# Routing slots of a two-branch layer: row units, wide comparisons, and a shifted job pair

## The reference

```python
xn = _layernorm(x, axis=-1)
x = x + attn(xn, ...) + ffn(xn, ...)

# attention branch: 16-channel tokens, qkv, windows of 8, depthwise conv, projection, norm
qkv = (tok @ qkv_w).reshape(B, -1, 3, C)
out = softmax(q * scale @ k.T) @ v + lepe
# expert branch: 16 experts in 4 groups, the best 6 of the best 2 groups
scores = sigmoid(hs @ gate_weight.T)
topk_idx, topk_weight = _gate(hs, gate_weight, bias)
for e in range(16):
    out += comb[:, e:e + 1] * ((silu(hs @ gate_proj[e].T) * (hs @ up_proj[e].T)) @ down_proj[e].T)
shared = (silu(hs @ shared_gate_w.T) * (hs @ shared_up_w.T)) @ shared_down_w.T
```

## Time and profile before

| | us |
|---|---|
| median of 3 runs (449.79 to 452.23) | 451.97 |
| span of the profiled execution | 455.0 |
| PE busy | 400.8 (88%) |
| VectorE busy | 364.8 (80%) |
| GpSimd busy | 234.7 (52%) |
| ScalarE busy | 224.8 (49%) |
| mean granted PE clock | 0.951 of full speed |

### The profile page before, as it was taken

How to read it: one execution, slowest core, us unless ns; L and a number is a source line. 1 busy time by engine, 2 the same in 40 slices (tenths; PEclk the granted TensorE clock), 3 DMA queues, 4 the chain that set the end, 5 groups by cost and what they waited for, 6 DMA issues and landing times.

```text
span 455.0 us, 7300 instructions
## 1 busy us (share of the span) xinstructions
PE 400.8 (88%) x1989; PEld 310.2 (68%) x1989; DVE 364.8 (80%) x593; ACT 224.8 (49%) x616; POOL 234.7 (52%) x221
## 2 busy tenths in 40 slices
PE   7799599999999999997999999989989999999200
PEld 7688499889767677675777777767667777767200
DVE  2869953686899989999799999999995355479951
ACT  3654234325564445653476864675437744554200
POOL 3530156775777777873000000007787777778671
PEclk9889979999999999999899999999999999999755
DMA  7998422226455766576733334336657997665652
GB/s 169 330 412 354 163 107 88 98 76 223 132 184 190 205 207 197 184 229 184 216 114 103 97 95 121 103 90 169 196 166 202 287 234 194 175 198 160 201 151 81
DMA packets 55878, 80.55 MB, mean 177 GB/s; under 512 B 8480, under 2 KB 47264, under 8 KB 55584
## 3 DMA queue, kind: packets, MB, share of 16 engines
q1 hardware_dynamic: 42912, 50.91, 36.7%
q0 software_dynamic: 9216, 25.96, 18.8%
q10 hardware_dynamic: 3712, 3.21, 2.4%
HBM read 43.48 MB, written 36.57 MB: 176 GB/s over the span
## 4 chain that ended last, share of the span: by engine, by line
PE 49%; DVE 22%; issue 12%; DMA 5%; POOL 4%; ACT 2%; SPq 2%; ACTq 1%; DVEq 1%; POOLq 0%
PE gate L991 15%; PE ps_y L1014 10%; POOL xs_dram L594 4%; PE ps_y L942 4%; DVE prod L1094 4%; DVE qkv L1094 4%; PE up L920 3%; PE ps_y L1007 3%; DVE inter_s L1532 3%; PE up L981 3%; DVE sc L1094 2%; PE gate L920 2%; DVE yacc L1614 2%; PE misc L882 2%; PE misc L1041 2%
## 5 line engine op out<-in xcount | busy, mean ns | idle before, releaser
L991 PE MATMUL gate<-wrec,xgT 128*128 x444 | 151.3, 463 | 2.9 <-ACT xgT L725 1.8
L594 POOL DMA_INDIRECT xs_dram<-xrow,slot_i x96 | 111.4, 1160 | 50.6 <-DMA xs_dram<-xrow,slot_i 21.5
L1014 PE MATMUL ps_y<-wrec,interT 88*128 x444 | 115.2, 382 | 0.0
L614 POOL DMA_INDIRECT gat<-y_dram,slot_i x50 | 55.0, 1099 | 113.6 <-DMA y_dram<-y_s 98.9
L991 PEld LDWEIGHTS gate<-wrec,xgT 128*128 128x128 f32 x444 | 75.8, 190 | 28.2 <-issue 4.4
L1014 PEld LDWEIGHTS ps_y<-wrec,interT 88*128 88x128 f32 x444 | 76.0, 191 | 6.7 <-issue 0.3
L1532 DVE SCALAR_TENSOR_TENSOR inter_s<-gate,xg,gate_s 128x176 f32<-128x176 f32 x111 | 43.6, 393 | 33.8 <-ACT gate_s L733 32.9
L733 ACT ACTIVATE gate_s<-gate 128x176 f32<-128x176 f32 x111 | 35.2, 317 | 70.1 <-PE ps_y L1007 67.7
L753 ACT ACTIVATE y_s<-ps_y 128x256 f32<-128x256 f32 x107 | 41.0, 383 | 55.7 <-PE up L981 52.6
L1007 PEld LDWEIGHTS ps_y<-ident,inter_s 128*88 128x88 f32 x222 | 26.7, 123 | 37.6 <-issue 19.3
L1007 PE MATMUL ps_y<-ident,inter_s 128*88 128x128 f32 x222 | 42.7, 274 | 5.0 <-DVE y_s L1556 2.8
(11 more groups left out here) (215 smaller groups left out, 633.8 us busy)
## 6 DMA issues: line engine op xcount, KB each, us to landing
xg<-xs_dram SPq DMA_DIRECT2D x111, 136.0 KB, 2.6
y_dram<-y_s SPq DMA_DIRECT2D x111, 128.0 KB, 2.1
wrec<-wexp SPq DMA_DIRECT2D x14, 608.0 KB, 15.1
xs_dram<-zrow SPq DMA_DIRECT2D x1, 2176.0 KB, 13.0
xn_dram<-xrow SPq DMA_DIRECT2D x8, 256.0 KB
qkv<-xn_dram SPq DMA_DIRECT2D x8, 256.0 KB
xs_dram<-xrow,slot_i POOLq DMA_INDIRECT x96, 2.9
wrec<-wexp SPq DMA_DIRECT2D x1, 1216.0 KB, 5.6
```

Of the source, the lines that this page charges most:

```text
L594: nc.gpsimd.indirect_dma_start(xs_dram[0:DONE[max(d for d in DONE if d <= c)] * P, :], bass.IndirectOffsetOnAxis(slot_i[:, o:o + 1], 0), x ...
L614: nc.gpsimd.indirect_dma_start(places[place_of(n)][:, there:there + H], None, y_dram[0:DONE[max(d for d in DONE if d <= first)] * P, :], b ...
L991: last = nc.tensor.matmul(guA[t % 2][:, 0:2 * I], xgT[:, t % 2, k * P:(k + 1) * P], wrec[:, bass.ds(record + k * 2 * I, 2 * I)], start=(k ...
L1014: last = nc.tensor.matmul(ps_y[:, t % 2 * 2 * H:t % 2 * 2 * H + H], interT[:, t % 2, k * P:(k + 1) * P], wrec[0:HALF, bass.ds(record + KT ...
```

## The change

The counts of rows are rounded down to whole tiles in units of rows (an AND with 4096 - 128) where they were shifted right to units of tiles and multiplied by 128 later; the lane table becomes 128 times the lane. `pads_ok` comes after one piece of `routing()`, which does without three multiplications. The slots are computed by `slots_of` with one instruction for all six later parts, first for columns 0 to 3 and then for columns 4 to 15. `JOBS_BEHIND` puts the five job pairs into steps 0, 2, 3, 4 and 5 where they were in steps 0 to 4. `LO_POOL` goes from 2 to 1, so `lo(1)` is VectorE's; on VectorE `lo` now stands ahead of the routing pieces of its unit.

```diff
+WHOLE_TILES = 4096 - P
+JOBS_BEHIND = (0, 2, 3, 4, 5)
-LO_POOL = 2
+LO_POOL = 1
-ROUTE_PLAN = {-1: 23, 0: 1, 1: 18, 2: 14, 3: 12, 4: 12}
+ROUTE_PLAN = {-1: 23, 0: 1, 1: 1, 2: 8, 3: 1, 4: 12}
...
-    if s not in range(5):
+    if s not in JOBS_BEHIND:
         return (), (), ()
-    n = FIRST_JOBS + 2 * s
+    n = FIRST_JOBS + 2 * JOBS_BEHIND.index(s)
...
-            nc.gpsimd.iota(lane_f[:, :], [[0, 1]], base=0, channel_multiplier=1,
+            nc.gpsimd.iota(lane_f[:, :], [[0, 1]], base=0, channel_multiplier=P,
...
-                do(nc.vector.tensor_scalar(whole[:, :], whole[:, :], 7, None, ALU.logical_shift_right))
+                do(nc.vector.tensor_scalar(whole[:, :], whole[:, :], WHOLE_TILES, None, ALU.bitwise_and))
...
-                tt(shift[:, every_part], begin[:, every_part], upto[:, 0:PARTS * NE], ALU.subtract)
-                yield
-                later = slice(2 * NE, (PARTS + 1) * NE)
-                tt(work[:, later], shift[:, later], shift[:, NE:PARTS * NE], ALU.subtract)
-                do(nc.vector.tensor_scalar(tiles[:, NE:PARTS * NE], upto[:, NE:PARTS * NE], float(P), None, ALU.mult))
-                settle(1)
-                do(nc.vector.tensor_scalar(shift[:, NE:2 * NE], shift[:, NE:2 * NE], float(P), 1.0, ALU.mult, ALU.add))
-                settle()
-                do(nc.vector.tensor_scalar(work[:, later], work[:, later], float(P), None, ALU.mult))
-                yield
+                settle()
+                do(nc.vector.scalar_tensor_tensor(shift[:, every_part], begin[:, every_part], 1.0, upto[:, 0:PARTS * NE],
+                                                  ALU.add, ALU.subtract))
+                tt(work[:, later], shift[:, later], shift[:, sooner], ALU.subtract)
...
-                for n, to in enumerate(beyond):
-                    do(nc.vector.tensor_tensor(ce(to), pos, every(tiles, n + 1), ALU.is_ge))
                     yield
...
+                def slots_of(c0, c1):
...
+                    do(nc.vector.tensor_tensor(runs, pos.unsqueeze(1).to_broadcast([P, n_e, wide, NE]), parts_of(upto[:, sooner]),
+                                               ALU.is_ge))
+                    do(nc.vector.tensor_tensor(slot, pos, shift[:, NE:2 * NE].unsqueeze(1).to_broadcast([P, wide, NE]), ALU.add))
+                    yield
+                    settle(1)
+                    do(nc.vector.tensor_tensor(runs, runs, parts_of(work[:, later]), ALU.mult))
+                    yield
+                    settle()
+                    do(nc.vector.tensor_tensor(runs[:, 0:3], runs[:, 0:3], runs[:, 3:6], ALU.add))
+                    yield
+                    settle()
+                    do(nc.vector.tensor_tensor(slot, slot, runs[:, 0], ALU.add))
+                    do(nc.vector.tensor_tensor(runs[:, 1], runs[:, 1], runs[:, 2], ALU.add))
+                    tt(slot, slot, runs[:, 1], ALU.add)
+                    tt(slot, slot, chosen[:, c0 * NE:c1 * NE].rearrange("p (c e) -> p c e", e=NE), ALU.mult)
+                    yield
...
+                for c0, c1 in ((0, 4), (4, TOK)):
+                    for _ in slots_of(c0, c1):
                         yield
...
+                if u > LO_POOL:
+                    lo(u - 1)
                 for _ in range(ROUTE_PLAN.get(u, 0)):
                     next(route, None)
-                if u > LO_POOL:
-                    lo(u - 1)
```

More of the change, by code:

```diff
@@ L1291, in routing @@
                 yield
+                later, sooner = slice(2 * NE, (PARTS + 1) * NE), slice(NE, PARTS * NE)
                 tt(tiles[:, every_part], upto[:, every_part], upto[:, 0:PARTS * NE], ALU.subtract)
@@ L1311, in routing @@
                 do(nc.vector.tensor_tensor(inner.rearrange("p (n e) -> p n e", e=NE),
[L1312 removed]
+                                           upto[0:1, sooner].rearrange("p (n e) -> p n e", e=NE),
                                            upto[0:1, PARTS * NE:].unsqueeze(1).to_broadcast([1, PARTS - 1, NE]), ALU.is_lt))
[L1314 removed]
+                do(nc.vector.tensor_scalar(base, upto[0:1, PARTS * NE:], float(P), None, ALU.max))
                 tt(inner, inner, work[0:1, later], ALU.mult)
@@ L1334, in routing @@
[L1334 to L1338, removed]
-                    yield
-                settle(3)
-                do(nc.vector.tensor_tensor(ce(TWO), ce(TWO), ce(beyond[0]), ALU.add))
-                do(nc.vector.tensor_tensor(ce(beyond[1]), ce(beyond[1]), ce(beyond[2]), ALU.add))
@@ L1354, in routing, with parts_of @@
-                tt(area(TWO, 256), area(TWO, 256), chosen, ALU.mult)
-                yield
-                settle()
-                for c in range(TOK):
-                    do(nc.vector.max(area(EIGHT + c * KEEP, KEEP), ce(TWO)[:, c, :]))
-                    if c % 4 == 3:
-                        some = slice((c - 3) * KEEP, (c + 1) * KEEP)
-                        settle()
-                        nc.vector.tensor_scalar(slot_i[:, some], area(EIGHT + some.start, 4 * KEEP), -1.0, None, ALU.add
-                                                ).then_inc(slots_ok, 1)
+                def slots_of(c0, c1):
+                    wide, n_e = c1 - c0, PARTS - 1
+                    runs = area(0, n_e * wide * NE).rearrange("p (n c e) -> p n c e", n=n_e, c=wide)
+                    slot = ce(TWO)[:, c0:c1, :]
+                    pos = misc[0][:, c0 * NE:c1 * NE].rearrange("p (c e) -> p c e", e=NE)
+                    def parts_of(ap):
+                        return ap.rearrange("p (n e) -> p n e", e=NE).unsqueeze(2).to_broadcast([P, n_e, wide, NE])
+                    settle()
+                    do(nc.vector.tensor_tensor(runs, pos.unsqueeze(1).to_broadcast([P, n_e, wide, NE]), parts_of(upto[:, sooner]),
+                                               ALU.is_ge))
+                    do(nc.vector.tensor_tensor(slot, pos, shift[:, NE:2 * NE].unsqueeze(1).to_broadcast([P, wide, NE]), ALU.add))
+                    yield
+                    settle(1)
+                    do(nc.vector.tensor_tensor(runs, runs, parts_of(work[:, later]), ALU.mult))
+                    yield
+                    settle()
[7 more added lines that the diff above has]
+                    yield
+                    settle()
+                    for c in range(c0, c1):
+                        do(nc.vector.max(area(EIGHT + c * KEEP, KEEP), ce(TWO)[:, c, :]))
+                        if c % 4 == 3:
+                            some = slice((c - 3) * KEEP, (c + 1) * KEEP)
+                            settle()
+                            nc.vector.tensor_scalar(slot_i[:, some], area(EIGHT + some.start, 4 * KEEP), -1.0, None, ALU.add
+                                                    ).then_inc(slots_ok, 1)
+                            yield
```

15 lines of the change are left out of this document (removed).

## The result

The changed kernel takes 453.98 us (median of 20 runs, 450.61 to 459.99) against 452.01 for the kernel before (20 runs, 448.68 to 458.53): a ratio of 1.006, 95% interval 1.0034 to 1.0086. Two repeats of the unchanged text gave 1.0031 [0.9984, 1.0078] and 1.0012 [0.9972, 1.0053], with 12 runs each. Ratios and intervals use only the runs that are no more than 1.5% above the fastest of their kernel. The medians of all runs in the two repeats, 454.31 against 454.85 us and 454.63 against 455.04, even lie 0.4 to 0.5 us the other way. So the change costs between nothing and about 0.6%, where 0.3% faster was forecast, and the two repeats alone show no change at all. Runs of either kernel spread over 7 to 13 us in every set, and the sets of the experiments were run on five different chips.

A forecast was written before the change was run, and what follows sets the result against it. The scatter stream behind `pads_ok` and the pad zeros was taken to set the end; shortening the pad rows shifts it 1.5 us, PE's lead buying nothing: 451.97 - 1.5 = 450.5 us, range 446.8 to 453.5.

The forecast's parts named there:

- The path: From `pads_ok` through pad zeros, first scatter and 96 scatters to tile 39: this sets the end, the stream taking 150.3 us.
- four columns first: Slot order on VectorE: needed so slots don't become later than the zeros; buys nothing more, first scatter at 57.71.
- Pad rows: Routing on VectorE before `pads_ok`: three multiplications removed, 1.51 us gained, with 0.4 as the low end.
- The job pair: Early PE stage: the 5.60 us stop and half clock go; PE gets 5.2 us of 8.4, bounds 3 to 6.
- two new stops: PE waiting for VectorE near 58 and 64 us, at `down(2)` and `down(3)`: 1.1 and 2.1 us.
- The stream in its new place: The 96 scatters on GpSimd: the whole stream shifts 1.5 us earlier, bounds 0.7 to 2.3.
- slow 15 us: Seven scatters around the end of the shared units, 2.17 us each: one event that only moves.
- rival 2: Earlier attention slows ten scatters, costing 2.6 us less 1.5: up to 1.1 us slower, typically zero; 0.16 shared with another rival.
- stop of 4 us before tile 15: PE, with its lead, would stand still some 4 us before tile 15, waiting for scatter 54.
- Rival 3: PE's slow clock after a new stop near tile 15 makes it late at tile 39: up to 455.0 us; chance 0.11.
- The base and the range: Whole kernel: 451.97 us as the start, range 446.8 to 453.5, about 0.5% (2.3 us) told from no change.

The follow-up runs named there:

- i1: Changed kernel with VectorE's lower attention quota (1.75 operations a tile instead of 1.9) kept for more tiles; 1.0135 of the kernel before, 459.08 us.
- g3: Changed kernel with most attention products and their sums on VectorE left out, so attention's result is not computed; 0.9716 of the kernel before, 441.14 us.
- f1: Changed kernel with four small GpSimd instructions put ahead of the first scatter as a delay; 1.0099 of the kernel before, 459.36 us.
- h2: Kernel before with its seven attention steps one unit earlier, in units 6 to 10 in place of 7 to 11; 1.0035 of the kernel before.
- g1: Changed kernel run once more without edit, for a third profile; 1.0012 of the kernel before, 454.63 us.
- f4: Kernel before with only the job pairs moved, to steps 0, 2, 3, 4 and 5; 1.0032 of the kernel before.
- e2: Changed kernel run again without edit, for a second profile; 1.0031 of the kernel before, 454.31 us.
- g2: Kernel before with three scatters in flight from the first on, instead of from the 40th; 0.9884 of the kernel before, 448.97 us.
- h4: Kernel before with three scatters in flight from the first on, run again on another occasion; 0.9914 of the kernel before, 449.18 us.
- h1: Changed kernel with attention steps moved to units 9 to 11 and the last weights' load held behind scatter 30; 1.002 of the kernel before.
- f3: Changed kernel with three scatters in flight from the first on, instead of from the 40th; 0.9835 of the kernel before, 447.53 us.
- e4: Changed kernel with the job pairs back in steps 0 to 4; 1.0035 of the kernel before.
- f2: Changed kernel with the seven attention steps of the shared units moved to units 9 to 11; 0.9977 of the kernel before.

## Why the prediction was off

**The path: right.** Zeros bind the first scatter of after, the slots are ready earlier (4.8 us behind the pad rows, where 53.2 - 48.5 = 4.7 to 55.5 - 48.5 = 7.0 was the estimate), and the stream sets the end. Nothing shows that "four columns first" was needed: in before the first slots were 1.0 us ahead of the first scatter, and they follow the pad rows too. From the last scatter to the end it is 243.8 to 247.2 us in every profile with two in flight, but for i1 and g3, whose attention differs; f1 and the four kernels with three in flight moved the stream and the time with it.

**Pad rows: the term mis-sized, by a collision taken for a duration.** 1.51 us was taken, 0.4 named as low end. Against undisturbed profiles it is 26.7 - 26.3 = 0.4 us. The prediction read in the earlier trace rows that L1305 ended with GpSimd's `lo`, so it had seen that 1.07 of 1.27 us was a meeting of two instructions; the step that failed was to count it as present in every execution. Of six profiles two have it, so on average the step is worth some 0.4 + 1.0 / 3 = 0.7 us, an estimate. L1305 takes 1.27 and 1.28 us in before and h2, where GpSimd's `lo` had begun 0.09 and 0.08 us ahead of it, and 0.21 us in the other four, where `lo` began 1.5 us behind it. By what means the one holds up the other no profile shows.

**The job pair: right in what it gives PE, up to tile 0.** There is no stop at 51. The end of the shared units, marked by SyncE's issue of the last weights' load, comes 66.6 to 67.3 us behind the start of routing in the three profiles of after, and 71.0 and 72.8 in the two of before: a lead of 3.7 to 6.2 us, where 5.2 was taken. Of the two new stops one appeared (1.01 at `down(3)`, 2.1 expected), the one near 58 did not. But tile 0's gate products come at 81.7, 82.4 and 83.6 against 85.2 and 83.4 us: on the means 1.7 us of the lead are left there.

**The stream in its new place: this failed.** The prediction took 1.5 us earlier for the whole stream and let its slow 15 us "only move". Instead the first 40 scatters take 65.3, 67.7 and 68.4 us in the three profiles of after, against 66.1 and 64.1 in the two of before: 2.0 us more on the means, against 0.4 to 0.7 us won at the start. That is rival 2 ("the gain is swallowed"), with two parts. One it had named, attention earlier on VectorE, priced at 2.6 us for ten scatters; scatters 1 to 21 took 3.6 us longer (32.3 against 28.7 on the means). The other it had dismissed: the weights' load, once behind scatter 30, now meets scatters 27 to 30 and holds up tile 0. In the stream it takes and gives: 21 to 31 are 2.0 us longer (18.8 against 16.8), 31 to 41 3.6 us shorter (16.0 against 19.6). The end of the shared units is not one event that moves: what it meets is different when PE moves and GpSimd does not. On the means the last scatter then comes 0.9 us earlier by its start, 2.0 later by the first 40 and 0.6 earlier by 41 to 96, in all 0.5 us later behind the start of routing, where 1.5 us earlier was forecast; profiles of one kernel differ by 5 us in the same sum. In short, the term of 1.5 us failed at both ends: the start moved by less, and the stream did not keep its length.

**Tile 15 and the clock.** A stop of 4 us before tile 15 was expected and none came: PE's lead was used up at tile 0, which waits for the late scatter 30 and then runs at a granted clock of 0.50, 2.71 us for four gate products that took 1.45. (g1 has 0.77 us before tile 15, f4 3.40.) Rival 3 had the slow clock, at the wrong tile; its 455.0 us is not what the profiles show. The slow clock lasts two tiles: from tile 0's gate products to tile 2's it is 5.71 us in after, 2.90 in before, so it costs PE 2.8 us. In spite of that PE still waits 1.60 to 3.01 us at tile 39 in the three profiles of after, so it costs the end nothing. Nor do the profiles show the two such stops between tiles 15 and 39 that rival 3 counted on: between tile 0 and 240 us the granted clock falls once in after and e2, at tile 0 (0.50), and in g1 a second time, behind its stop of 3.01 us at tile 39 (0.61 over 4.4 us).

**The base and the range.** 451.97 was a median of three runs of a kernel that spreads over 10 us; the sets of before since then gave medians from 452.01 to 456.78. The measured 453.98 lies 0.5 us above the upper end of the forecast range, 453.5, which had no room for the spread of the base. For the same reason 0.5% was too fine a bound: three measurements of one pair of kernels gave 1.006, 1.003 and 1.001.

**Open.** What makes the spread of some 10 us. In the profiles with two in flight it sits mainly in scatters 41 to 96 (79.7 to 89.5 us, without g3) and in the stage before routing (28.6 to 31.5). Scatters in step with VectorE are part of it in four profiles, but no run removed them by themselves. With three in flight the twelve runs of g2 and of h4 spread over only 3.7 and 4.1 us, beside 12.4 and 13.3 us of before (23 and 29 runs) in the same sets, so most of the spread goes when the stream no longer sets the end. And how much of the small loss in time is due to the stretched first 40 scatters: h1 mended them and did not become faster by anything that could be measured.

## What to carry to other kernels

Find the stream that sets the end, and try how many of its transfers are in flight before shortening what leads to it: one constant gave 0.9 to 1.6% against before in both kernels, more than this whole change moved. An instruction that is long only because it met another, as L1305 was in two of six profiles (1.27 and 1.28 us, against 0.21 in four), is an event with a frequency; take a second profile of the unchanged kernel before putting it into a sum. And when one engine gets a lead, write down which transfers and which long instructions come forward with it (here the load of 1.2 MB and the products of 1024 elements), and what they will meet in the stream that does not.

## What the runs showed of the hardware

- In after a GpSimd scatter instruction takes no more than 0.97 us in 56 of 96 cases, and up to 2.68 us beside VectorE's products and sums of 1024 elements (3.38 in f3): 7 of the 67 that overlap a TENSOR_TENSOR of 1024 elements take 1.9 us or more, and none of the other 29 takes more than 1.35. Leaving most products out (g3) took the excess over 0.96 us of all 96 scatters from 17.6 to 5.4 us, and the stream became 6.6 us shorter.
- The two engines fell in step at the end of the stream in four profiles (e4, f1, f2, h2), one scatter of 2.27 or 2.28 us per VectorE tile of 2.58 us, and PE then stood idle for 6.65 to 9.36 us at tile 39, while before's profile has none of it in the same stretch (scatters of 0.95 to 1.54 us, PE idle for 3.02).
- In after one load of 1.2 MB stretched the landing of a scatter beside it from 2.5 to 5.65 us. In after, e2, g1 and f4 GpSimd waits 3.4 to 4.6 us for a landing beside that load.
